# Second selective scan: the order of three instructions on TensorE and ScalarE in steps 3 and 4 of each group of eight

## The chip, the cores and the metric

One core of a Trainium2 chip. The time is the device time of one execution in microseconds (us); the kernel before was run three times.

## The reference, cut to what matters

The program is a chain of four layers on a tensor of 8 x 64 x 32 x 32: window attention with an MLP, an up- and down-sampling filter, a two-way selective scan over 8 tokens of each pixel ("scan 2"), and a selective scan over 1024 positions with an MLP ("scan 3"). The change lies in the second scan alone:

```python
def step(hst, inp):
    d_t, u_t, B_t, C_t = inp
    dA = jnp.exp(d_t[:, :, None] * A)
    hst = dA * hst + (d_t * u_t)[:, :, None] * B_t[:, None, :]
    y_t = jnp.einsum('bdn,bn->bd', hst, C_t)
    return (hst, y_t)
```

It runs over 8 tokens forward and, for the reversed sequence, backward. Here d is delta, the softplus of a projection; u is the projected input; B and C have 16 states; A is 16 x 16.

## The kernel before, in words

`scan2` (L888) works in 128 units. Eight units make a group (512 columns of pixels and tokens), and a unit covers 1024 columns of 128 (channel, state) pairs. Five engines run the same software pipeline, each in its own instruction stream: step s is written out for 16 values of u (`skewed2`, L875), the first 16 and the last 16 steps are peeled, and the rest is a loop. k = u % 8 is the place of a step in its group. The order on an engine is the order of the statements in `body`; an engine waits on semaphores and nothing behind a waiting instruction goes ahead.

What a step does:

- TensorE (L944 on). It spreads one unit's input (`ps_u`, s_pu in the trace, four matmuls: two halves of 512 columns, each the sum of a high and a low part), which needs DVE's `feed` of the unit before (semaphore `fed`); in steps k = 3 and 4 it subtracts the high part of B or of C from what stands in `ps_m` (L957, one matmul with the negated identity); it spreads the unit's delta (`ps_d`, s_pd, four matmuls, L940 as all spreads); it spreads one half of B or C into `ps_m` (`states(0)`, two matmuls; in step 3 it waits for the low part of B, in step 4 for that of C), sums products over states into `ps_y` (L1003, 16 small matmuls), spreads the other half (`states(1)`), and in k = 0 to 3 computes a projection of the next group into the same `ps_m` (L1017 to L1027: xp, delta, B, C).
- ScalarE (L1037 on). In k = 3 and 4 it copies the remainder out of `ps_m` as the low part (L1063); it takes the exponentials `fore` (L1069) and `aft` (L1074) of the spread delta, the decays of the forward and of the backward scan, with the copy of the first half of B or C (`states(0)`, L1058) between them and that of the second half (`states(1)`) behind; then come the k-dependent copies for the next group (in k = 3 the high part of C L1104, the logarithm L1106 and exp minus 1 L1108; in k = 2 the high part of B L1098 and L1100).
- DVE (L1132 on). Per unit: `feed` = spread input x B (L1140), the forward scan `ahead` (L1147, needs `fore`), the backward scan `back` (L1150, needs `aft`).
- GpSimd (L1160 on). It issues the DMA that adds `back` onto `ahead` (L1176) and multiplies the sum by C (L1173); in k = 4 to 7 it finishes delta, input and their low parts for the next group (L1179 to L1200).

PSUM holds one copy each of `ps_u`, `ps_d` and `feed` (two banks each), and of `ps_m` and `ps_y`: `ps_m` is used by every spread of B and C, by both subtractions and by every projection, one after another.

TensorE is in step s with unit s - 8 for input and delta; ScalarE takes the decays of unit s - 8 in step s; DVE works on unit s - 9. In the peeled first steps (s below 8) there is no unit yet, and from s = 128 on there is no further group. So steps 3 and 4 hold both a subtraction and a unit for units 3 and 4, 11 and 12, and so on to 115 and 116: 15 pairs, the first of them in the run-in, where the sums over states (L1003) have not begun.

Of the kernel before, what the change touches and what calls it, by code (L numbers as in the profile page):

```python
# [10 lines left out]
ACT = mybir.ActivationFunctionType  # L11
# [55 lines left out]
def live(p, n):  # L67

    return not isinstance(p, int) or 0 <= p < n
# [801 lines left out]
UNITS = 128  # L871
# [16 lines left out]
def scan2(nc, consts, x, xt, y, selr, ysel):  # L888
# [6 lines left out]
    with ExitStack() as ctx:  # L895
# [7 lines left out]
        negid = m.sb("s_negid", [P, P], F32R)  # L903
        parts_b, parts_c, parts_d, parts_u = (m.sb("s_parts" + t, [P, 2, 2, N], F32R) for t in "bcdu")
# [5 lines left out]
        ps_m, ps_y = (m.banks("s_p" + t, 1)[0] for t in "my")  # L910
# [3 lines left out]
            log_done, delta_done, du_done, b_rest, c_rest = (m.sem("s_" + t) for t in (  # L914
                "xpps", "xpd", "dtps", "bps", "cps", "awayd", "relud", "exd", "oned", "lnd", "grownd", "offd",
                "logd", "deltad", "dud", "brest", "crest"))
        hi_d, hi_u, hi_b, hi_c, lo_d, lo_u, lo_b, lo_c = (
            m.sem("s_" + t) for t in ("hid", "hiu", "hib", "hic", "lod", "lou", "lob", "loc"))
# [15 lines left out]
        @block.tensor  # L934
        def _(pe):
            pe.wait_ge(ready, 5)

            def spread(bank, sel, parts):
                for part in range(2):
                    mm = pe.matmul(bank, selr[:, sel * P:(sel + 1) * P], parts[:, part], start=(part == 0),  # L940
                                   stop=(part == 1))
                return mm

            def body(s, u):  # L944
                k, par, gi = u % 8, u // 8, s - u % 8
                p, v = s - LAG_D, u - LAG_D
                if live(p, UNITS):
                    half, j, g = place(v)
                    if v % 8 == 0:
                        pe.wait_ge(lo_u, p + 8)  # L950
                    wait(pe, fed, p)
                    for i in range(2):
                        mm = spread(ps_u[:, i * N:(i + 1) * N], 2 * (2 * j + i) + g, parts_u[:, half])
                    mm.then_inc(u_rep, 1)
                if k in (3, 4) and live(s, UNITS):
                    pe.wait_ge((hi_b, hi_c)[k - 3], gi + 8)
                    pe.matmul(ps_m[:], negid[:], (parts_b, parts_c)[k - 3][:, par, 0], start=False, stop=True,  # L957
                              skip_group_check=True).then_inc((b_rest, c_rest)[k - 3], 8)
                if live(p, UNITS):
                    if v % 8 == 0:  # L960
                        pe.wait_ge(lo_d, p + 8)
                    wait(pe, fore_done, p)
                    wait(pe, aft_done, p)
                    for i in range(2):
                        mm = spread(ps_d[:, i * N:(i + 1) * N], 2 * (2 * j + i) + g, parts_d[:, half])
                    mm.then_inc(d_ps, 1)
                q, w = s - LAG_B, u - LAG_B

                def states(i):
                    half, j, second = place(w)  # L970
                    if w % 8 == second and i == 0:
                        pe.wait_ge((lo_b, lo_c)[second], q - second + 8)
                    if i == 1:
                        pe.wait_ge((b_copied, c_copied)[second], q - second + 1)
                    else:
                        if isinstance(q, int) and q == 0:
                            pe.wait_ge(lo_c, 8)
                        if 1 <= k <= 4 and live(s, UNITS):
                            pe.wait_ge((xp_done, relu_done, lo_b, lo_c)[k - 1], gi + 8)
                        if second:  # L980
                            pe.wait_ge(b_copied, q + 1)
                        else:
                            wait(pe, c_copied, q)
                    spread(ps_m[:], 16 + 2 * j + i, (parts_b, parts_c)[second][:, half]).then_inc(
                        (b_rep, c_rep)[second], 1)

                if live(q, UNITS):
                    states(0)
                o = s - LAG_Y
                if live(o, UNITS):  # L990
                    _, j, g = place(u - LAG_Y)
                    if (u - LAG_Y) % 8 == 0:
                        wait(pe, y_done, o)
                        off = 8 * o if isinstance(o, int) else o * 8
                        for h in range(HALVES):
                            px = x[:].rearrange("p (b n) -> p b n", n=HW)[:, :, ds(off, PX)]
                            pe.matmul(ps_y[:].rearrange("p (b h n) -> p h b n", h=HALVES, n=PX)[:, h], wskip[:, h], px,
                                      start=(h == 0), stop=False, skip_group_check=True)
                    pe.wait_ge(prod_done, o + 1)
                    terms = prod[:, (u - LAG_Y) % 2].rearrange("p (n t) -> p t n", t=TOK)  # L1000
                    for odd in range(2):
                        for quad in range(4):
                            mm = pe.matmul(ps_y[quad * 32:(quad + 1) * 32, j * NPX:(j + 1) * NPX],  # L1003
                                           ysel[:, (2 * odd + g) * 32:(2 * odd + g + 1) * 32],
                                           terms[:, 2 * quad + odd], start=False, stop=(odd == 1 and g == 1),
                                           tile_position=(0, quad * 32), skip_group_check=True)
                    mm.then_inc(y_part, 1)
                if live(q, UNITS):
                    states(1)
                if k < 4 and live(s, UNITS):  # L1010
                    if live(q, UNITS):
                        if w % 2:
                            pe.wait_ge(c_copied, q + 1)
                        else:
                            pe.wait_ge(b_copied, q + 2)
                    if k == 0:
                        pe.matmul(ps_m[:], c["wxp"][:, par * P:(par + 1) * P], xt[:, ds((s - u) * 32, N)],  # L1017
                                  start=True, stop=True).then_inc(xp_ps, 8)
                    if k == 1:
                        pe.wait_ge(xp_done, gi + 8)  # L1020
                        pe.matmul(ps_m[:], wdt[:], xp[:], start=True, stop=True).then_inc(dt_ps, 8)
                    if k == 2:
                        pe.wait_ge(relu_done, gi + 8)
                        pe.matmul(ps_m[:], c["wb"], xp[:], start=True, stop=True).then_inc(b_ps, 8)
                    if k == 3:
                        pe.wait_ge(lo_b, gi + 8)
                        pe.matmul(ps_m[:], c["wc"], xp[:], start=True, stop=True).then_inc(c_ps, 8)  # L1027

            skewed2(pe, body)

        @block.scalar
        def _(act):
# [4 lines left out]
            def body(s, u):  # L1037
# [8 lines left out]
                p, v = s - LAG_D, u - LAG_D  # L1046
# [3 lines left out]
                def states(i):  # L1050
                    second, buf = w % 2, w % (4 + 4 * (w % 2)) // 2
                    if live(q, UNITS):
                        act.wait_ge((b_rep, c_rep)[second], q - second + i + 1)
                        if second:
                            wait(act, prod_done, q - 7)
                        else:
                            wait(act, fed, q - 2)
                        act.activation((bs, cs)[second][:, buf, i], ps_m[:],  # L1058
                                       ACT.Copy).then_inc((b_copied, c_copied)[second], 1)

                if k in (3, 4) and live(s, UNITS):
                    act.wait_ge((b_rest, c_rest)[k - 3], gi + 8)
                    act.activation((parts_b, parts_c)[k - 3][:, par, 1], ps_m[:],  # L1063
                                   ACT.Copy).then_inc((lo_b, lo_c)[k - 3], 8)
                if live(p, UNITS):
                    b, g = v % 2, place(v)[2]
                    act.wait_ge(d_ps, p + 1)
                    wait(act, ahead_done, p - 1)
                    act.activation(fore[:, b, :, 1:], rates[:, :, 1:], ACT.Exp,  # L1069
                                   scale=aneg[:, g:g + 1]).then_inc(fore_done, 1)  # L1070
                states(0)
                if live(p, UNITS):
                    wait(act, back_done, p - 1)
# [728 lines left out]
```

## Time and profile before

| what | value |
|---|---|
| median of 3 runs | 2016.04 us (2014.6 to 2017.21) |
| the profiled execution's own time | 2014.68 us |
| its span in the trace | 2012.7 us |
| share of the span: TensorE, DVE, ScalarE, GpSimd busy | 82%, 79%, 58%, 58% |
| first and last `feed` of the second scan | 509.0 and 1258.9 us |
| mean granted TensorE clock | 0.942 of full speed |

The span is what the trace covers; 1.98 us of the execution lie around it. The share of busy time is a mean over stages with different limits, so the scan is read by itself, between 509 and 1265 us, in order of time. A bracket behind a row gives the idle time of the engine just before the instruction and what released it.

### The profile page before, as it was taken

Reading aid. Unit: us, or ns where it says so; the run is one execution under the profiler, and the core shown is the slowest. Engines: PE = TensorE matmul, PEld = TensorE weight load, DVE = VectorE, ACT = ScalarE, POOL = GpSimd, SP = SyncE. Lnnn points to the kernel's source line nnn. Section 1 sums busy time; section 2 is a strip of 40 time slices with the busy share of each in tenths; the row PEclk is TensorE's granted clock in tenths of the full one; section 3 lists DMA queues with packets and bytes.
Section 4 is the critical chain, followed back from the end, with each engine's and each line's share of the span. In section 5 each row is a group of like instructions: output and inputs, shape, how many; then the busy total and the mean of one; then the engine's idle time right before and its main releaser. Section 6 shows DMA issues by size and latency. Waiting matters only on the chain. (4 is left out here: it accounts for less than half of the span.)

```text
span 2012.7 us, 31048 instructions
## 1 busy us (share of the span) xinstructions
PE 1651.0 (82%) x9878; PEld 979.8 (49%) x9878; DVE 1585.5 (79%) x1549; ACT 1158.2 (58%) x1889; POOL 1168.7 (58%) x881
## 2 busy tenths in 40 slices
PE   5888787996788888888888888657888888888787
PEld 2555444884444454444545544234555554554333
DVE  3788745554799999999999999441899999999854
ACT  3444484334666666666666665265666665665356
POOL 0666501001467767676776775202899999999701
PEclk8999988997899999999999999777999999999898
DMA  4000000000254444444444444200000000000001
GB/s 135 2 0 0 1 0 1 1 1 1 53 95 88 90 90 87 94 83 94 89 89 83 94 91 92 44 1 0 1 1 0 0 0 0 0 0 0 7 5 42
DMA packets 23435, 78.21 MB, mean 39 GB/s; under 512 B 3792, under 2 KB 4816, under 8 KB 23120
## 3 DMA queue, kind: packets, MB, share of 16 engines
q0 software_dynamic: 18432, 67.12, 17.6%
q1 hardware_dynamic: 4944, 10.35, 1.8%
q8 instruction: 32, 0.52, 0.1%
q14 instruction: 27, 0.22, 0.0%
HBM read 8.25 MB, written 2.10 MB: 5 GB/s over the span
## 5 line engine op out<-in xcount | busy, mean ns | idle before, releaser
L1173 POOL TENSOR_TENSOR s_prod<-s_ahead,s_cs 128x1024 f32<-128x1024 f32 x128 | 312.2, 2439 | 203.7 <-DVE s_back L1150 103.1
L1708 POOL TENSOR_TENSOR r_prod<-r_state,r_cs 128x512 f32<-128x512 f32 x256 | 322.4, 1298 | 14.8 <-DVE r_state L1649 14.2
L1147 DVE TENSOR_TENSOR_SCAN s_ahead<-s_fore,s_pfeed 128x1024 f32<-128x1024 f32 x128 | 292.7, 2287 | 11.8 <-ACT s_fore L1069 5.3
L1150 DVE TENSOR_TENSOR_SCAN s_back<-s_aft,s_pfeed 128x1024 f32<-128x1024 f32 x128 | 289.5, 2261 | 0.0
L1069 ACT ACTIVATE s_fore<-s_pd,s_aneg 128x896 f32<-128x896 f32 x128 | 129.7, 1013 | 161.0 <-PE s_pd L940 161.0
L940 PE MATMUL s_pu<-s_partsu,selr 128*128 128x512 f32 x512 | 173.4, 462 | 52.2 <-DVE s_pfeed L1140 52.0
L1636 DVE TENSOR_TENSOR r_feed<-r_pu,r_bs 128x512 f32<-128x512 f32 x256 | 164.4, 687 | 61.9 <-PE r_pu L1478 61.9
L1140 DVE TENSOR_TENSOR s_pfeed<-s_pu,s_bs 128x1024 f32<-128x1024 f32 x128 | 157.8, 1233 | 37.7 <-PE s_pu L940 25.0
L1601 ACT ACTIVATE r_decay<-r_pd,r_aneg 128x512 f32<-128x512 f32 x256 | 168.3, 686 | 23.2 <-PE r_pd L1478 23.0
L1478 PE MATMUL r_pu<-r_parts,selr 128*128 128x512 f32 x512 | 161.3, 437 | 5.7 <-DVE r_feed L1636 5.7
L1649 DVE TENSOR_TENSOR_SCAN r_state<-r_decay,r_carry,r_feed 128x512 f32<-128x512 f32 x128 | 156.3, 1263 | 0.0
L1478 PE MATMUL r_pd<-r_parts,selr 128*128 128x512 f32 x512 | 154.5, 405 | 0.0
L1003 PE MATMUL s_py<-s_prod,ysel 128*32 128x128 f32 x2048 | 142.4, 408 | 12.2 <-POOL s_prod L1173 12.2
L940 PEld LDWEIGHTS s_pu<-s_partsu,selr 128*128 128x128 f32 x512 | 95.0, 194 | 117.5 <-DVE s_pfeed L1140 73.0
L1649 DVE TENSOR_TENSOR_SCAN r_state<-r_decay,r_feed 128x512 f32<-128x512 f32 x128 | 148.6, 1202 | 0.0
L940 PE MATMUL s_pd<-s_partsd,selr 128*128 128x512 f32 x512 | 144.9, 407 | 0.0
L1478 PE MATMUL r_pm<-r_parts,selr 128*128 128x512 f32 x256 | 92.2, 443 | 57.1 <-POOL r_parts L1713 45.8
L1074 ACT ACTIVATE s_aft<-s_pd,s_aneg 128x896 f32<-128x896 f32 x128 | 129.8, 1014 | 0.0
L1478 PEld LDWEIGHTS r_pu<-r_parts,selr 128*128 128x128 f32 x512 | 93.9, 193 | 72.0 <-issue 39.2
L1176 POOL DMA_DIRECT2D s_ahead<-s_back x128 | 120.3, 940 | 14.6 <-DVE s_back L1150 14.6
L940 PEld LDWEIGHTS s_pd<-s_partsd,selr 128*128 128x128 f32 x512 | 101.0, 197 | 21.9
L1478 PEld LDWEIGHTS r_pd<-r_parts,selr 128*128 128x128 f32 x512 | 99.0, 193 | 25.1 <-issue 1.0
(255 smaller groups left out, 3338.1 us busy)
## 6 DMA issues: line engine op xcount, KB each, us to landing
s_ahead<-s_back POOLq DMA_DIRECT2D x128, 512.0 KB, 4.5
x_act<-in_x_dram SPq DMA_DIRECT2D x8, 256.0 KB, 5.4
out_dram<-x_act SPq DMA_DIRECT2D x16, 128.0 KB, 2.3
k_scan<-in_pack_scan_dram SPq DMA_DIRECT2D x1, 1600.0 KB, 10.4
k_fir<-in_pack_fir_dram SPq DMA_DIRECT2D x1, 1600.0 KB, 13.8
k_l<-in_pack_l_dram SPq DMA_DIRECT2D x1, 450.0 KB, 6.9
k_ln<-in_pack_ln_dram SPq DMA_DIRECT2D x3, 131.0 KB, 3.0
k_mlp<-in_pack_mlp_dram SPq DMA_DIRECT2D x2, 194.0 KB, 5.1
```

What stands on the lines that cost most here:

```text
L940: mm = pe.matmul(bank, selr[:, sel * P:(sel + 1) * P], parts[:, part], start=(part == 0), stop=(part == 1))
L1003: mm = pe.matmul(ps_y[quad * 32:(quad + 1) * 32, j * NPX:(j + 1) * NPX], ysel[:, (2 * odd + g) * 32:(2 * odd + g + 1) * 32], terms[:, 2 * ...
L1074: act.activation(aft[:, b, :, :TOK - 1], rates[:, :, :TOK - 1], ACT.Exp, scale=aneg[:, g:g + 1]).then_inc(aft_done, 1)
L1140: dve.tensor_tensor(feed[:], ps_u[:], bs[:, buf].rearrange("p i n -> p (i n)"), ALU.mult).then_inc(fed, 1)
L1147: dve.tensor_tensor_scan(ahead[:, v % 4], f, feed[:], 0.0, ALU.mult, ALU.add).then_inc(ahead_done, 1)
L1150: dve.tensor_tensor_scan(back[:, v % 4, ::-1], a[:, ::-1], feed[:, ::-1], 0.0, ALU.mult, ALU.add).then_inc(back_done, 1)
L1173: pool.tensor_tensor(prod[:, b], ahead[:, v % 4], cs[:, buf].rearrange("p i n -> p (i n)"), ALU.mult).then_inc(prod_done, 1)
L1478: mm = pe.matmul(bank[:], selr[:, sel * P:(sel + 1) * P], parts[:, par, which, part], start=(part == 0), stop=(part == 1))
L1601: act.activation(decay[:, v % 2, q], ps_d[q % 2][:], ACT.Exp, scale=aneg[:, v % 4:v % 4 + 1]).then_inc(decayed, 1)
L1636: dve.tensor_tensor(feed[q % 2][:], ps_u[q % 2][:], bs[:, lc, q], ALU.mult).then_inc(fed, 1)
L1649: dve.tensor_tensor_scan(state[:, b, q], decay[:, b, q], feed[q % 2][:], start, ALU.mult, ALU.add).then_inc(scanned, 1)
L1708: pool.tensor_tensor(prod[:, v % 2, q], state[:, v % 2, q], cs[:, v % UNROLL // 4, q], ALU.mult).then_inc(multiplied, 1)
```

## The change

On TensorE the spread of delta goes ahead of the subtraction of the high parts; on ScalarE the forward decays (`fore`) go ahead of the copy of the low parts. Both concern only steps k = 3 and k = 4. Nothing is added or removed, and every wait goes with its instruction.

```diff
@@ TensorE
                         mm = spread(ps_u[:, i * N:(i + 1) * N], 2 * (2 * j + i) + g, parts_u[:, half])
                     mm.then_inc(u_rep, 1)
-                if k in (3, 4) and live(s, UNITS):
-                    pe.wait_ge((hi_b, hi_c)[k - 3], gi + 8)
-                    pe.matmul(ps_m[:], negid[:], (parts_b, parts_c)[k - 3][:, par, 0], start=False, stop=True,
-                              skip_group_check=True).then_inc((b_rest, c_rest)[k - 3], 8)
-                if live(p, UNITS):
                     if v % 8 == 0:
                         pe.wait_ge(lo_d, p + 8)
                     wait(pe, fore_done, p)
...
                     mm.then_inc(d_ps, 1)
+                if k in (3, 4) and live(s, UNITS):
+                    pe.wait_ge((hi_b, hi_c)[k - 3], gi + 8)
+                    pe.matmul(ps_m[:], negid[:], (parts_b, parts_c)[k - 3][:, par, 0], start=False, stop=True,
+                              skip_group_check=True).then_inc((b_rest, c_rest)[k - 3], 8)
@@ ScalarE
-                if k in (3, 4) and live(s, UNITS):
-                    act.wait_ge((b_rest, c_rest)[k - 3], gi + 8)
-                    act.activation((parts_b, parts_c)[k - 3][:, par, 1], ps_m[:],
-                                   ACT.Copy).then_inc((lo_b, lo_c)[k - 3], 8)
                 if live(p, UNITS):
...
                     act.activation(fore[:, b, :, 1:], rates[:, :, 1:], ACT.Exp,
                                    scale=aneg[:, g:g + 1]).then_inc(fore_done, 1)
+                if k in (3, 4) and live(s, UNITS):
+                    act.wait_ge((b_rest, c_rest)[k - 3], gi + 8)
+                    act.activation((parts_b, parts_c)[k - 3][:, par, 1], ps_m[:],
+                                   ACT.Copy).then_inc((lo_b, lo_c)[k - 3], 8)
                 states(0)
```

## Rows read from the trace of the kernel before

**Rows 1.** A stretch: us, busy of PE, PEld, DVE, ACT, POOL, PEclk, DMA share, GB/s

```profile
880.00:890.00 10.00, 8.41 (x51) 5.07 (x49) 9.76 (x6) 4.36 (x7) 5.50 (x5) 0.83 0.55 105
```

**Rows 2.** The page's costliest groups: busy, mean ns, idle before and its main releaser

```profile
L1147 DVE TENSOR_TENSOR_SCAN s_ahead<-s_fore,s_pfeed 128x1024 f32<-128x1024 f32 x128 | 292.7, 2287 | 11.8 <-ACT s_fore L1069 5.3
```

**Rows 3.** Timeline (start, us, engine, line), DVE, from 901 us

```profile
901.00 1.23 DVE L1140 TENSOR_TENSOR s_pfeed<-s_pu,s_bs 128x1024 f32<-128x1024 f32 x1
...
906.84 1.23 DVE L1140 TENSOR_TENSOR s_pfeed<-s_pu,s_bs 128x1024 f32<-128x1024 f32 x1
...
908.11 2.29 DVE L1147 TENSOR_TENSOR_SCAN s_ahead<-s_fore,s_pfeed 128x1024 f32<-128x1024 f32 x1
...
910.31 2.26 DVE L1150 TENSOR_TENSOR_SCAN s_back<-s_aft,s_pfeed 128x1024 f32<-128x1024 f32 x1
...
914.48 2.29 DVE L1147 TENSOR_TENSOR_SCAN s_ahead<-s_fore,s_pfeed 128x1024 f32<-128x1024 f32 x1 [0.57 <-ACT s_fore L1069]
```

**Rows 4.** Timeline, TensorE and ScalarE in a step k = 1

```profile
892.15 1.50 PE L940 MATMUL s_pu<-s_partsu,selr 128*128 128x512 f32 x4
...
893.48 1.07 PE L940 MATMUL s_pd<-s_partsd,selr 128*128 128x512 f32 x4
...
894.60 1.01 ACT L1069 ACTIVATE s_fore<-s_pd,s_aneg 128x896 f32<-128x896 f32 x1 [1.20 <-PE s_pd L940]
```

**Rows 5.** Timeline, TensorE and ScalarE in a step k = 3

```profile
904.14 1.48 PE L940 MATMUL s_pu<-s_partsu,selr 128*128 128x512 f32 x4
...
905.53 0.48 PE L957 MATMUL s_pm<-s_partsb,s_negid 128*128 128x512 f32 x1
...
906.11 0.60 ACT L1063 ACTIVATE s_partsb<-s_pm 128x512 fp32r<-128x512 f32 x1 [0.20 <-PE s_pm L957]
...
906.77 0.72 PE L940 MATMUL s_pm<-s_partsb,selr 128*128 128x512 f32 x2
...
906.97 1.01 ACT L1069 ACTIVATE s_fore<-s_pd,s_aneg 128x896 f32<-128x896 f32 x1 [0.27 <-PE s_pd L940]
...
907.42 1.11 PE L1003 MATMUL s_py<-s_prod,ysel 128*32 128x128 f32 x16
907.88 0.59 ACT L1058 ACTIVATE s_bs<-s_pm 128x512 f32<-128x512 f32 x1
...
908.35 1.01 ACT L1074 ACTIVATE s_aft<-s_pd,s_aneg 128x896 f32<-128x896 f32 x1
...
908.52 0.73 PE L940 MATMUL s_pm<-s_partsb,selr 128*128 128x512 f32 x2
...
910.52 1.50 PE L940 MATMUL s_pu<-s_partsu,selr 128*128 128x512 f32 x4
```

**Rows 6.** Timeline, TensorE and ScalarE in the step k = 4 behind it

```profile
913.39 1.00 ACT L1069 ACTIVATE s_fore<-s_pd,s_aneg 128x896 f32<-128x896 f32 x1
...
914.22 1.11 PE L1003 MATMUL s_py<-s_prod,ysel 128*32 128x128 f32 x16
...
915.26 0.73 PE L940 MATMUL s_pm<-s_partsc,selr 128*128 128x512 f32 x2
...
915.83 0.40 PE L940 MATMUL s_pu<-s_partsu,selr 128*128 128x512 f32 x1
```

**Rows 7.** Timeline, a DVE feed and TensorE's spread of input behind it, before steps k = 3

```profile
807.38 1.23 DVE L1140 TENSOR_TENSOR s_pfeed<-s_pu,s_bs 128x1024 f32<-128x1024 f32 x1
...
808.95 1.50 PE L940 MATMUL s_pu<-s_partsu,selr 128*128 128x512 f32 x4
...
854.30 1.23 DVE L1140 TENSOR_TENSOR s_pfeed<-s_pu,s_bs 128x1024 f32<-128x1024 f32 x1
...
855.69 1.50 PE L940 MATMUL s_pu<-s_partsu,selr 128*128 128x512 f32 x4
```

**Rows 8.** Timeline, GpSimd's last piece for a group, and the spread that needs it

```profile
880.61 1.73 POOL L1200 TENSOR_TENSOR s_partsu<-s_du,s_partsu 128x512 fp32r<-128x512 f32 x1
...
884.87 1.94 PE L940 MATMUL s_pu<-s_partsu,selr 128*128 128x512 f32 x4 [1.50 <-DVE s_pfeed L1140]
```

## The prediction

> **What bounds the kernel now.** I read first how full each engine is in a stretch of the second scan. DVE is busy 9.76 of 10 us there [rows 1], so the scan goes at DVE's pace, and a change on TensorE or ScalarE counts only where DVE has to wait. The page tells how much there is to win: before all 128 forward scans DVE sat idle 11.8 us, and 5.3 us of it ended with the forward decays `fore` [rows 2]. Then I read DVE's own order of time [rows 3]: one unit takes 5.84 us (feed at 901.00, the next at 906.84); the forward scan begins 1.27 us after the feed does, the backward scan 2.20 us after that. One stall stands there: at 914.48 the forward scan had waited 0.57 us for `fore`, which had ended at 914.39 [rows 6], so 0.09 us lie between an end on ScalarE and the start on DVE that it frees. This stall costs 0.53 us against the regular pace, and I found it twice in the steady part, both in a step k = 4.
>
> Last I read how late TensorE begins a unit. Its spread of the input may start when DVE's feed of the unit before ends; call the distance the lag. In steps k = 3 it is 0.16 us (855.69 after 855.53), 0.34 us (808.95 after 808.61) [rows 7] or 1.91 us (904.14 after 902.23) [rows 3, 5]. Of the 14 groups behind the run-in six lie at 0.07 to 0.16 (0.83 together), five at 0.33 or 0.34 (1.68), one at 1.30 and two at 1.91: 7.63 us in all. TensorE and ScalarE have a cycle of their own in these steps, because `ps_m` is handed back and forth: in k = 3 spread to spread takes 6.38 us (904.14 to 910.52) [rows 5], in k = 4 5.31 us (to 915.83) [rows 6]. So k = 3 loses 0.54 us to DVE and k = 4 wins 0.53 back. That is the slack on which the change works.
>
> **Step k = 3 in the new order**, times from the start of the input spread. The delta spread no longer stands behind the subtraction. It starts as in k = 1, at 893.48 - 892.15 = 1.33, and ScalarE begins `fore` at 894.60 - 892.15 = 2.45 [rows 4]; before it was 906.97 - 904.14 = 2.83 [rows 5]. So `fore` comes 0.38 us earlier, which is the change's gain. The subtraction (0.48 us [rows 5]) follows on TensorE and is over by about 2.9, while `fore` runs: it costs nothing, and its cover is `fore`. But the low part waits on ScalarE behind `fore`. From one ScalarE instruction to the next it goes 907.88 - 906.97 = 0.91 behind a `fore`, so the low part starts at 3.36 and ends 0.60 later, at 3.96; before it ended at 2.57. Queued behind it, on both engines:
> - states(0) on TensorE, 0.06 after it (906.77 after 906.71): 4.02, over at 4.74; before 2.63.
> - The sums over states, 0.65 later: 4.67; before 3.28.
> - The copy of B's first half, 0.10 after the spread's end, as the low part stands behind the subtraction (906.11 after 906.01): 4.84; before 3.74.
> - `aft`, 0.47 behind that copy: 5.31 to 6.32; before 4.21 to 5.22.
> - states(1) stands behind the sums, which hold TensorE 1.04 us (914.22 to 915.26 [rows 6]): 5.71; before 4.38.
> - From states(1) to the next input spread 2.00 us pass (908.52 to 910.52): 7.71 instead of 6.38.
>
> So this step grows by 1.33 us. Before, the low part was copied while TensorE spread delta; now two waits in series that lay beside each other have become one chain.
>
> **Step k = 4.** The same holds up to states(1): `fore` at 2.45 (ScalarE's copies for the next group are over by 2.49, within the overlap of its instructions), `aft` from 5.31 to 6.32, states(1) at 5.71. From there the next input spread takes 0.57 us (915.26 to 915.83 [rows 6]), so the step takes 6.28 us instead of 5.31.
>
> **What DVE sees.** Let L be the lag at k = 3. At k = 4 it is L + 7.71 - 5.84 = L + 1.87. Counted from the end of the feed before, DVE wants its feed at 5.84 - 1.23 = 4.61, the forward scan at 5.88 and the backward scan at 8.08 [rows 3]. In k = 4:
> - The input spread ends at L + 1.87 + 1.50: in time for L below 1.24.
> - `fore` ends at L + 1.87 + 3.46 = L + 5.33, plus 0.09: the forward scan is met for L below 0.46.
> - `aft` ends at L + 1.87 + 6.32, plus 0.09 = L + 8.28. DVE wants it at 8.08. **The backward scan waits L + 0.20 us in every group.**
>
> The waits are one behind another, so the last one counts, not their sum. In k = 5 the lag of a group with L = 0.34 is about 2.1, no instruction is late any more, and TensorE has made the rest good by k = 7, where today it stands waiting for DVE (1.50 us at 884.87 [rows 8]). Over 14 groups: 7.63 + 14 x 0.20 = 10.4 us. The two stalls of today are in that (they are the groups with L = 1.91), so 2 x 0.53 = 1.1 us goes off: **+9.3 us**.
>
> The edits with one answer: no DMA is moved, and SP's queue is not touched. GpSimd's chain for the next group starts from ScalarE's last copy of k = 4, which comes 1.33 us later; its last piece ended at 882.34 and TensorE took it at 884.87 [rows 8], 2.5 us of cover, which remains. Were that gone, the rest (at most 1.33 us less DVE's own delay) would fall on k = 0. In the run-in the sums over states are still missing, DVE does wait for `fore` there, and `fore` comes 0.4 us earlier twice, while `aft` and the next spread come later: I take zero, with -1 and +1.5 as ends. The last steps hold no such pair.
>
> The terms that no row shows are where the handovers fall in the new order. From below: if the sums let states(1) through as soon as its copy is done, it starts at 5.5, L + 0.20 becomes about L - 0.05, and the total +5. From above: the two handovers from TensorE to ScalarE may take the 0.27 us that ScalarE waited for delta [rows 5] instead of 0.10, in two steps, some 0.4 us per group: +15. I take the middle value, since each of its pieces has a row of the same pair of instructions.
>
> The profiled execution took 2014.68 us; with +9.3 it would take 2024.0. It lies 1.36 us below the median of the three runs, 2016.04, so that I forecast 2016.04 + 9.3 = **2025.3 us**.
>
> **The clock.** In the stretch at 880 to 890 us the granted clock was 0.83, so part of it at 1.2 and part at 2.4 GHz [rows 1]; TensorE had waited 1.50 us for DVE just before its input spread, and this spread took 1.94 us instead of 1.50 [rows 4, 8]. This group is the one with L = 1.91. So one such stretch at an unlucky place costs 1.6 us of lag, of which DVE felt only 0.53; with the slack gone it would feel all.
> The Trainium skill ("TensorE: Matmul & The Clock Gate", "HAM oscillation — how this bites in real kernels") says that a TensorE that idles between bursts falls back to the slow clock again and again. The trace agrees so far as the one stretch shows. By that rule the new waits for the low parts, some 1.4 us each, would bring more slow stretches than today.
>
> **Rivals.**
> - *More slow stretches.* If each of the other 11 groups got one at the bad place: 11 x 1.6 = 18 us more, 2043 us. For it: TensorE idles longer in k = 3 and 4. Against it: it idles less in k = 5 to 7, where most of its waiting lies now, and its work is the same. Chance 0.08.
> - *The chain is hidden.* If the pieces overlap better by over half a microsecond per group, only the three groups with a long lag stall: 1.0 + 1.6 + 1.6 - 1.1 = +3.1 us, 2019.1 us, or about nothing. Against it: ScalarE keeps its order, and both `fore` and `aft` (2 x 1 us) and two copies have to pass. Chance 0.13.
> - *Faster: `fore` is what decides.* The backward scan always finds `aft` ready, as it does today, and all idle time that ended with `fore`, 5.3 us [rows 2], goes: 2010.7 us. It decides if `aft` ends before 8.08, that is if the low part, states(0) and its copy take at least 0.2 us less than I add up even in groups with the smallest lag, and over 1.9 us less in the late ones; also most of the 5.3 us lies in steps of the run-in that aren't touched. Chance 0.04.
> - *The change does not do what it says*, because in k = 4 `fore` stands behind ScalarE's copies that end at 2.49: this touches 0.04 us, and would leave the losses. It is within the forecast.
>
> **How the numbers follow.** The forecast has 0.75. A measurement of this kernel can tell about 0.2%, 4 us. The forecast's own ends, +5 to +15, give 2021 to 2031; to hold the time 8 times in 10 I reach to 2019 for the hidden chain and to 2033 for one or two more slow stretches. Slower by over 0.2%: 0.75 + 0.08 = 0.83, and with a little of the hidden chain's chance 0.84; within 0.2%: 0.12; faster by over 0.2%: 0.04.
>
> **What would show it.** In the changed profile: `fore` at 2.45 after the input spread in k = 3 and 4; the low part directly behind it; 7.7 and 6.3 us from input spread to input spread; a new line of idle time before the backward scan (today 0), ended by `aft`, some 0.3 to 0.5 us per group in k = 4, and no stall before the forward scan in the steady part. If the backward scan has no idle time the forecast is wrong, and so it is if TensorE's cycle in k = 3 stays under 7 us.

## The result, and the profile of the changed kernel

The changed kernel takes 2030.51 us (median of 6 runs, 2028.4 to 2032.29) against 2015.13 us for the kernel before in the same series: 15.4 us more, ratio 1.0075 with a 95% interval of 1.0062 to 1.0088. The forecast was 2025.3 us, 9.3 us more than before, so the measured time lies 5.2 us above it, inside the stated range of 2019 to 2033.

The page of the changed kernel has this span and these lines for the two scans (busy, mean ns, idle before and its main releaser):

```profile
span 2030.4 us, 31048 instructions
...
L1146 DVE TENSOR_TENSOR_SCAN s_ahead<-s_fore,s_pfeed 128x1024 f32<-128x1024 f32 x128 | 292.7, 2287 | 13.8 <-ACT s_fore L1064 7.4
L1149 DVE TENSOR_TENSOR_SCAN s_back<-s_aft,s_pfeed 128x1024 f32<-128x1024 f32 x128 | 289.9, 2265 | 6.9 <-ACT s_aft L1073 6.9
```

The view of who waited for whom, DVE in the second scan (us in total, times, longest):

```profile
DVE s_pfeed L1139 <- PE s_pu L940: 30.5, 7, 24.9
DVE s_ahead L1146 <- ACT s_fore L1064: 7.4, 11, 1.5
DVE s_back L1149 <- ACT s_aft L1073: 6.9, 16, 0.6
```

Before, the forward scan had waited 5.3 us for `fore` [rows 2]. The third line is the announced new one: the backward scan, which never had to wait, now waits 16 times for `aft`. 16 is 14 steady groups and the two units of the run-in (the peeled first steps). The 11 waits before the forward scan are six of the run-in and one of about 0.63 us in each of five groups that TensorE began late. In the first line the 24.9 us are the wait for the very first input (23.2 before); the other six waits, 5.6 us, are for an input spread that came late.

The steps themselves. The timeline of a regular group, k = 3 from 865.35 and k = 4 from 873.05, TensorE, ScalarE and DVE:

```profile
865.35 1.49 PE L940 MATMUL s_pu<-s_partsu,selr 128*128 128x512 f32 x4
...
866.68 1.07 PE L940 MATMUL s_pd<-s_partsd,selr 128*128 128x512 f32 x4
...
867.60 0.39 PE L964 MATMUL s_pm<-s_partsb,s_negid 128*128 128x512 f32 x1
867.79 1.01 ACT L1064 ACTIVATE s_fore<-s_pd,s_aneg 128x896 f32<-128x896 f32 x1 [0.68 <-PE s_pd L940]
868.70 0.59 ACT L1068 ACTIVATE s_partsb<-s_pm 128x512 fp32r<-128x512 f32 x1
869.34 0.73 PE L940 MATMUL s_pm<-s_partsb,selr 128*128 128x512 f32 x2 [1.36 <-ACT s_partsb L1068]
...
870.01 1.11 PE L1002 MATMUL s_py<-s_prod,ysel 128*32 128x128 f32 x16
870.11 0.60 ACT L1057 ACTIVATE s_bs<-s_pm 128x512 f32<-128x512 f32 x1 [0.82 <-PE s_pm L940]
870.61 1.01 ACT L1073 ACTIVATE s_aft<-s_pd,s_aneg 128x896 f32<-128x896 f32 x1
...
871.05 0.73 PE L940 MATMUL s_pm<-s_partsb,selr 128*128 128x512 f32 x2
...
873.05 1.49 PE L940 MATMUL s_pu<-s_partsu,selr 128*128 128x512 f32 x4
...
875.50 1.01 ACT L1064 ACTIVATE s_fore<-s_pd,s_aneg 128x896 f32<-128x896 f32 x1
...
878.38 1.01 ACT L1073 ACTIVATE s_aft<-s_pd,s_aneg 128x896 f32<-128x896 f32 x1
...
879.33 0.85 PE L940 MATMUL s_pu<-s_partsu,selr 128*128 128x512 f32 x3
879.52 2.29 DVE L1149 TENSOR_TENSOR_SCAN s_back<-s_aft,s_pfeed 128x1024 f32<-128x1024 f32 x1 [0.34 <-ACT s_aft L1073]
```

From the input spread on, `fore` comes at 2.44 (forecast 2.45, before 2.83 [rows 5]), the low part at 3.35 (3.36), states(0) (the spread of the first half) at 3.99 (4.02), its copy at 4.76 (4.84), `aft` at 5.26 (5.31), states(1) at 5.70 (5.71), and the next input spread at 7.70 (7.71, before 6.38). Step k = 4 takes 6.28 us, as forecast (873.05 to 879.33). Two brackets show the price: TensorE stands 1.36 us for the low part, and ScalarE 0.82 us for states(0), in a stretch where both had gone on before. `aft` of k = 4 ends at 879.39, and the backward scan begins at 879.52.

Where the time went, by the two profiled executions (feed times from DVE's timeline). In the 14 steady groups steps 3 and 4 cost DVE 12.9 us over the regular 5.84 per unit, against 1.0 before: +11.9. The units 0 to 5 took 42.7 us from first feed to seventh, against 40.7: +2.1. The other 3.7 us of the 17.7 us between the spans (2.2 before the first feed, 1.5 behind the last) lie in code that the change doesn't touch; this execution also lay 1.8 us above its median. 11.9 + 2.1 = 14.0 us stands against the 15.4 us of the medians.

### The profile page after: what moved, and what is told of

The parts are those of the page before. It is cut to its first block and busy times, and to the rows that moved or that the text cites. A ratio compares the mean times of both kernels' runs of the same rounds, so it can differ in the third digit from the quotient of the medians.

```text
span 2030.4 us, 31048 instructions
## 1 busy us (share of the span) xinstructions
PE 1650.8 (81%) x9878; PEld 986.8 (49%) x9878; DVE 1587.1 (78%) x1549; ACT 1161.9 (57%) x1889; POOL 1168.7 (58%) x881
## 3 DMA queue, kind: packets, MB, share of 16 engines
q0 software_dynamic: 18432, 67.12, 17.5%
## 5 line engine op out<-in xcount | busy, mean ns | idle before, releaser
L1707 POOL TENSOR_TENSOR r_prod<-r_state,r_cs 128x512 f32<-128x512 f32 x256 | 323.4, 1303 | 15.9 <-DVE r_state L1648 15.4
L940 PE MATMUL s_pm<-s_partsb,selr 128*128 128x512 f32 x256 | 89.9, 433 | 31.3 <-ACT s_partsb L1068 20.4
## 6 DMA issues: line engine op xcount, KB each, us to landing
k_fir<-in_pack_fir_dram SPq DMA_DIRECT2D x1, 1600.0 KB, 14.1
```

The costliest lines, as they stand in the source:

```text
L1707: pool.tensor_tensor(prod[:, v % 2, q], state[:, v % 2, q], cs[:, v % UNROLL // 4, q], ALU.mult).then_inc(multiplied, 1)
```

## The experiments

A group is called late when its lag L at k = 3 is 1.3 us or more, and regular otherwise; to stall is to exceed DVE's 5.84 us per unit. Theory: steps 3 and 4 are one chain of handovers of `ps_m` between TensorE and ScalarE; the low part behind `fore` lengthens it, and DVE pays L plus a constant in k = 4, L being the lag at k = 3. The constant follows from the order alone. Rivals: only the late `aft` costs something; each moved instruction has a price of its own and the prices add up; the extra time is TensorE's clock.

**Step 3 alone, step 4 alone.**

```diff
@@ TensorE, ahead of delta's spread
+                if k == 4 and live(s, UNITS):
+                    pe.wait_ge(hi_c, gi + 8)
...
@@ TensorE, behind it
-                if k in (3, 4) and live(s, UNITS):
+                if k == 3 and live(s, UNITS):
...
@@ ScalarE, the same for the low part, around fore
```

This is step 3 alone against the changed kernel; in the other kernel 3 and 4 are exchanged.

> The new order in step k = 3 alone; k = 4 as before. Theory (chain over ps_m): TensorE's cycle is 7.71 us in k = 3 and stays 5.31 in k = 4, so the unit of k = 4 begins L + 1.87 us behind its gate, and its forward decays end at 3.87 instead of 3.46 after the spread of the input: the forward scan, not the backward one, waits L - 0.05 us per group, with L the lag at k = 3 (0.15 to 0.35 in most groups, 1.3 to 1.9 where the TensorE clock fell before the group). Sum over 14 groups, with the two stalls of before taken off, +6 to +8 us, and 1 us in the run-in: about 2022 us. Rival (only the late backward decays of k = 4 cost anything, k = 3 is covered by the slack): within 2 us of before.

Measured: 2024.84 us against 2015.34, ratio 1.0043 (1.0030 to 1.0055), six runs from 2018.5 to 2028.28. The waits of DVE:

```profile
DVE s_ahead L1155 <- ACT s_fore L1073: 10.2, 14, 2.0
...
DVE s_back L1158 <- ACT s_aft L1082: 0.5, 1, 0.5
```

The wait is before the forward scan, as expected, and not before the backward one. The lags at k = 3 in the profiled execution add up to 8.45 us; L - 0.05 over 14 groups gives 7.75, and 7.75 us were found. So the rival in which only a late `aft` costs falls: step 3 alone, whose own `aft` no steady scan waits for, costs 9.5 of the 15.4 us, in the steady groups through step 4's `fore` (and, in the four late ones, its input first). The median is 2.8 us above the expected 2022. In the profiled execution the steady groups cost 7.75 less the 1.0 of before, inside the expected 6 to 8; the run-in cost 2.1 us, not 1. The rest of the 2.8 us isn't located.

> The new order in step k = 4 alone; k = 3 as before. Theory: the cycle stays 6.38 us in k = 3 and is 6.28 in k = 4; the unit of k = 4 begins only L + 0.54 behind its gate, the backward decays end 6.32 later, and DVE waits L - 1.13 us, that is nothing in the regular groups and 0.3 to 0.8 in the two to five late ones; the two stalls of 0.53 before go. Together 0 to +2 us: about 2016 us, not to be told from before. Rival (each late low part costs the same, about half of the loss per step): +7 us.

Measured: 2018.88 us against 2015.34, ratio 1.0016 (1.0007 to 1.0025), where 0 to +2 us was expected. The ten regular groups stall 0.00 us. Four late groups, with L = 1.61, 1.61, 1.72 and 1.90, stall 0.49, 0.49, 0.66 and 0.76; L - 1.13 gives 0.48, 0.48, 0.59 and 0.77. The mechanism holds, and with four late groups the scan of the profiled execution is only 1.7 us longer than before, as expected; but this execution lies 1.9 us below its median, and what makes the median 3.5 us isn't shown; more late groups in the other executions could do it. The two steps together cost 15, alone 9.5 and 3.5: with step 3 as before, step 4's new order stays within the slack of a regular group; with step 3 in the new order the slack is gone, and it turns L - 0.05 into L + 0.20.

**The run-in alone, and everything but the run-in.**

```diff
@@ TensorE and ScalarE, at the new places
-                if k in (3, 4) and live(s, UNITS):
+                if k in (3, 4) and isinstance(s, int) and s < 16 and live(s, UNITS):
...
@@ TensorE and ScalarE, at the old places
+                if k in (3, 4) and not (isinstance(s, int) and s < 16) and live(s, UNITS):
...
```

In the other kernel the two conditions are exchanged.

> The new order only in the peeled first steps (s = 11 and 12, units 3 and 4). The theory on record had zero here; the trace of the changed kernel shows units 3 to 5 taking 23.4 us instead of 20.1. Theory now: DVE waits in the run-in for TensorE, so every us of longer cycle is paid in full (1.1 in k = 3) and the late spread of unit 4 falls into a longer stretch of the slow TensorE clock: +2 to +3.5 us, about 2018 us. Rival (the clock in the run-in differs from run to run anyway, and the order costs nothing): within 1 us of before.

Measured: 2018.02 us against 2015.34 (ratio 1.0015, 1.0006 to 1.0024), +2.7 us.

> The new order everywhere but in the peeled first steps. Theory: the 14 steady groups alone cost 12 us (L + 0.20 each, with the L of the changed kernel, 1.06 taken off): about 2027 us, and with the run-in's part it adds up to the whole change, +15. Rival (the steady part costs the +9.3 on record and the run-in the rest): 2024.5 us.

Measured: 2027.83 us, ratio 1.0060 (1.0047 to 1.0073), +12.5 us, where the theory had 12 and the rival 9.3. Together 15.2 us: the two parts make up the whole change. The profile is less clear than the time: its execution has three late groups, as before has, and its steady groups stall 10.6 us (L + 0.20 gives 10.1), 9.6 us more than before. It took 12.9 us more than the profiled execution before; 2.7 us of that lie ahead of the first feed and behind the last, in code that is the same.

What happens in the run-in stands in the timeline of the changed kernel, units 3 and 4:

```profile
528.40 1.49 PE L940 MATMUL s_pu<-s_partsu,selr 128*128 128x512 f32 x4
...
534.73 2.29 DVE L1149 TENSOR_TENSOR_SCAN s_back<-s_aft,s_pfeed 128x1024 f32<-128x1024 f32 x1 [0.49 <-ACT s_aft L1073]
...
536.73 2.69 PE L940 MATMUL s_pu<-s_partsu,selr 128*128 128x512 f32 x4
...
539.47 1.23 DVE L1139 TENSOR_TENSOR s_pfeed<-s_pu,s_bs 128x1024 f32<-128x1024 f32 x1 [2.45 <-PE s_pu L940]
...
542.16 2.29 DVE L1146 TENSOR_TENSOR_SCAN s_ahead<-s_fore,s_pfeed 128x1024 f32<-128x1024 f32 x1 [1.46 <-ACT s_fore L1064]
```

and in the kernel before, TensorE's input spreads of the same two units and of unit 5:

```profile
527.39 1.50 PE L940 MATMUL s_pu<-s_partsu,selr 128*128 128x512 f32 x4
...
534.13 2.69 PE L940 MATMUL s_pu<-s_partsu,selr 128*128 128x512 f32 x4
...
540.20 1.09 PE L940 MATMUL s_pu<-s_partsu,selr 128*128 128x512 f32 x4
```

There is no slack here: DVE waits in every one of these units, so the longer step is paid at once. From the spread of unit 3 to that of unit 4 it is 8.33 us instead of 6.74, and from there to unit 5 8.22 us (to 544.95) instead of 6.07. The slow spread of unit 4, 2.69 us, is not new: it took as long before. What the run-in costs hangs on where such slow stretches fall. The kernel with the sums first, below, has the changed kernel's order in this run-in and is slow at unit 3 instead of 4 (2.63 and 1.50 us); its units 0 to 5 took 40.8 us, against 42.7 in the changed kernel, 43.3 in the one with the run-in alone, and 40.7 and 41.1 in the two with the old order there. So +2.7 us is the difference of the medians, and in a single execution it can be next to nothing. The stretch 530 to 545 us, of the changed kernel (PE, PEld, DVE, ACT, POOL, then PEclk):

```profile
530.00:545.00 15.00, 10.18 (x25) 5.78 (x24) 9.79 (x7) 8.59 (x13) 8.09 (x6) 0.75 0.19 37
```

and of the kernel before:

```profile
530.00:545.00 15.00, 12.21 (x52) 7.44 (x51) 12.15 (x7) 10.57 (x15) 10.26 (x8) 0.89 0.19 37
```

The granted clock was 0.75 instead of 0.89, that is, more of the stretch at 1.2 GHz; TensorE had waited 1.36 us for the low part in step k = 3, shortly before. That this wait brought the clock down is not shown, and two kernels speak against it: with the sums first, where TensorE waits 1.35 us at the same place, the same stretch had 0.96, and with ScalarE's half alone 0.94.

**Each engine's half alone.**

```diff
@@ TensorE's half alone, against the changed kernel
+                if k in (3, 4) and live(s, UNITS):
+                    act.wait_ge((b_rest, c_rest)[k - 3], gi + 8)
+                    act.activation((parts_b, parts_c)[k - 3][:, par, 1], ps_m[:],
+                                   ACT.Copy).then_inc((lo_b, lo_c)[k - 3], 8)
                 if live(p, UNITS):
...
-                if k in (3, 4) and live(s, UNITS):
-                    act.wait_ge((b_rest, c_rest)[k - 3], gi + 8)
...
                 states(0)
```

ScalarE's half alone has TensorE's instructions back in the old order instead, and ScalarE as in the change.

> TensorE's half alone: delta's spread ahead of the subtraction, ScalarE still copies the low part ahead of the forward decays. Theory, from the start of the input spread: subtraction at 2.25, low part 2.74 to 3.34, forward decays 3.23 to 4.24, states(0) 3.40, its copy 4.20, backward decays 4.67 to 5.68, states(1) 5.09: cycle 7.09 us in k = 3 and 5.66 in k = 4; DVE waits max(0, L - 0.30) us for the forward decays in k = 4, so 0.05 in the regular groups and 1.0 to 1.6 in two to five late ones; with the run-in +3 to +6 us, about 2020 us. Rival (the moved subtraction is what costs): the full +15 us.

Measured: 2021.64 us against 2015.60, ratio 1.0037 (1.0024 to 1.0050), +6.0. Regular groups stall 0.00 to 0.02 us, four late ones (L = 1.83, 1.73, 1.88, 1.75) 1.52, 1.42, 1.55 and 1.41, with L - 0.30 giving 1.53, 1.43, 1.58 and 1.45.

> ScalarE's half alone: the forward decays ahead of the low part, TensorE still subtracts ahead of delta's spread. Theory: forward decays at 2.83, low part 3.74 to 4.34, states(0) 4.40, backward decays 5.69 to 6.70, states(1) 6.09: cycle 8.09 us in k = 3, 6.66 in k = 4; DVE waits L + 0.96 us for the backward decays in every group: 22 us in the steady part, 3 to 5 in the run-in: about 2040 us, dearer than the whole change. Rival (the two halves add up to the whole +15): about 2025 us.

Measured: 2037.66 us against 2015.60, ratio 1.0117 (1.0102 to 1.0131), +22.1, the dearest of all. DVE's timeline in its step 4:

```profile
829.48 1.23 DVE L1140 TENSOR_TENSOR s_pfeed<-s_pu,s_bs 128x1024 f32<-128x1024 f32 x1
831.37 2.29 DVE L1147 TENSOR_TENSOR_SCAN s_ahead<-s_fore,s_pfeed 128x1024 f32<-128x1024 f32 x1 [0.65 <-ACT s_fore L1065]
834.22 2.29 DVE L1150 TENSOR_TENSOR_SCAN s_back<-s_aft,s_pfeed 128x1024 f32<-128x1024 f32 x1 [0.57 <-ACT s_aft L1074]
836.61 1.23 DVE L1140 TENSOR_TENSOR s_pfeed<-s_pu,s_bs 128x1024 f32<-128x1024 f32 x1
```

All 14 groups pay: 7.13 us instead of 5.84 here (L = 0.32; L + 0.96 = 1.28, found 1.29), 17.5 us in all, with L + 0.96 giving 16.8. The expected 2040 us took late groups as in the changed kernel; this execution had none, only one slow stretch behind a step 4 that cost 0.7 us more. 6.0 + 22.1 is far from 15.4: the halves don't add up, since TensorE's half takes the subtraction out of `fore`'s way, 0.38 us in each of the two steps, and so turns the L + 0.96 of ScalarE's half into L + 0.20. That rival falls.

**Two changes to the changed kernel.**

```diff
@@ the sums first: TensorE
-                if live(q, UNITS):
+                if live(q, UNITS) and not (k in (3, 4)):
                     states(0)
                 o = s - LAG_Y
...
                     mm.then_inc(y_part, 1)
+                if live(q, UNITS) and k in (3, 4):
+                    states(0)
                 if live(q, UNITS):
                     states(1)
@@ the decays together: ScalarE
-                states(0)
+                if not (k in (3, 4)):
+                    states(0)
                 if live(p, UNITS):
                     wait(act, back_done, p - 1)
                     act.activation(aft[:, b, :, :TOK - 1], rates[:, :, :TOK - 1], ACT.Exp,
                                    scale=aneg[:, g:g + 1]).then_inc(aft_done, 1)
+                if k in (3, 4):
+                    states(0)
                 states(1)
```

> The changed kernel, but in steps 3 and 4 TensorE does the sums over states ahead of states(0), while it waits for the low part. Theory: states(1) no longer stands behind the sums but only behind the copy of the first half, at 5.48 instead of 5.71; cycle 7.48 us in k = 3 and 6.05 in k = 4; the wait in k = 4 falls from L + 0.20 to L - 0.03, 3.2 us in 14 groups: about 2027 us. Rival (the sums aren't on the path, ScalarE's order alone decides): no difference to the changed kernel, 2030.5 us.

Measured: 2029.72 us against 2015.60, ratio 1.0073 (1.0060 to 1.0086): 14.1 us above before and not to be told from the changed kernel. The theory had 2027 and misses; by the median the rival (no difference, 2030.5) is met. The trace tells two effects apart. In the regular groups the step is shorter, and DVE waits less: a group with L = 0.34 stalls 0.24 instead of 0.54 us, one with L = 0.15 some 0.1 instead of 0.43. Its step k = 3:

```profile
815.07 1.49 PE L940 MATMUL s_pu<-s_partsu,selr 128*128 128x512 f32 x4
...
817.63 1.11 PE L1002 MATMUL s_py<-s_prod,ysel 128*32 128x128 f32 x16
...
819.06 0.73 PE L940 MATMUL s_pm<-s_partsb,selr 128*128 128x512 f32 x2 [0.32 <-ACT s_partsb L1070]
...
820.49 0.73 PE L940 MATMUL s_pm<-s_partsb,selr 128*128 128x512 f32 x2 [0.69 <-ACT s_bs L1059]
...
822.48 1.48 PE L940 MATMUL s_pu<-s_partsu,selr 128*128 128x512 f32 x4
```

7.41 us instead of 7.70, and states(1) now waits for the copy, not for the sums. But six of the 14 groups met a slow stretch of TensorE's clock in this execution, five in the changed kernel's, and each cost about 1.77 us. Four of them have L = 0.15 or less, so that L - 0.03 doesn't foretell them: in all four the input spread of step 4 itself took 2.69 us instead of 1.49, and the granted clock around it (677.5 to 684.5 us for the first) was 0.76. So in this order, in the one execution profiled, the rival of the prediction, slow stretches that fall into steps 3 and 4, takes back what the shorter step wins.

> The changed kernel, but in steps 3 and 4 ScalarE takes the backward decays ahead of the copy of the first half, into the time in which it waits for states(0). Theory: backward decays 3.86 to 4.87 instead of 5.31 to 6.32, the copy of the first half still at 4.84, cycle still 7.71 and 6.28 us. DVE no longer waits for the backward decays; it waits max(0, L - 0.46) us for the forward ones and max(0, L - 1.05) for the feed: nothing in the regular groups, 1.0 to 1.5 us in two to five late ones; run-in still +1 to +3: about 2019 us. Rival (the longer cycle costs by itself, whichever decays are late): 2028 us or more.

Measured: 2023.41 us against 2015.60, ratio 1.0039 (1.0024 to 1.0053), six runs from 2019.21 to 2029.37. A step k = 3 of it on ScalarE, and the copy that follows:

```profile
814.42 1.01 ACT L1064 ACTIVATE s_fore<-s_pd,s_aneg 128x896 f32<-128x896 f32 x1 [0.67 <-PE s_pd L940]
815.32 0.59 ACT L1068 ACTIVATE s_partsb<-s_pm 128x512 fp32r<-128x512 f32 x1
815.80 1.02 ACT L1074 ACTIVATE s_aft<-s_pd,s_aneg 128x896 f32<-128x896 f32 x1
...
816.74 0.60 ACT L1057 ACTIVATE s_bs<-s_pm 128x512 f32<-128x512 f32 x1
```

`aft` fills what had been ScalarE's wait, the copy comes no later, and the step still takes 7.69 us (811.98 to 819.67). No backward scan waits any more, the eight regular groups stall 0.00 us, and the six late ones (L from 1.48 to 1.83) stall 1.00 to 1.35, with L - 0.46 giving 1.02 to 1.37. So about half of the loss (7.8 of 15.4 us are left) was `aft`'s place behind the copy; in a regular group the longer step does not cost by itself, and the rival (2028 us or more) falls by the median, though one single run lay at 2029.37. In a late group the longer step does cost. The median is 4.4 us above the expected 2019. The profiled execution had six late groups where I had taken two to five, at about 1.2 us each; another 4.3 us of it lie behind the last feed, in code that is the same, and there its granted clock was lower (0.97 in 1600 to 1800 us, against 1.00 in the matching 200 us of before). The single runs of this kernel differ by 10 us.

**A version meant to beat both**: step 3 as before, in step 4 the new order with both decays ahead of the copy; and the same with the sums first.

```diff
@@ TensorE and ScalarE: the new order for k == 4 alone, as above, and on ScalarE
-                states(0)
+                if not (k == 4):
+                    states(0)
...
+                if k == 4:
+                    states(0)
                 states(1)
```

> Step k = 3 as before; in k = 4 the new order, with the backward decays ahead of the copy of the first half as well. A try at a version that beats both. Theory: unit 4 of a group begins L + 0.54 behind its gate, forward decays end 3.46 and backward ones 4.87 later: DVE waits max(0, L - 1.79) us, so at most 0.1 in a late group instead of the 0.53 of before, and unit 4 of the run-in gets its forward decays about 0.4 us earlier: 0.5 to 2 us faster than before, about 2014 us, less than the measurement can tell; the profile shows it as idle time before the forward scans of 4 us or less instead of 5.3, and none before the backward scans. Rival (k = 4's longer cycle of 6.28 us costs by itself): as the order in k = 4 alone, 2018.9 us.

Measured: 2014.50 us against 2015.95, ratio 1.0001 (0.9992 to 1.0010), 11 runs, ten of them from 2013.86 to 2017.46 and one at 2023.13: no difference. The DVE waits of its profiled execution:

```profile
DVE s_pfeed L1151 <- PE s_pu L940: 26.4, 3, 24.9
DVE s_ahead L1158 <- ACT s_fore L1073: 5.7, 5, 1.5
```

No stall in any of the 14 steady groups, though two had L = 1.74 and 1.56; all five waits for `fore` lie in the run-in, and they came to 5.7 us in this execution, not to the 4 or less that were expected.

> The same, and in k = 4 TensorE does the sums over states ahead of states(0). Theory: cycle 6.05 instead of 6.28 us in k = 4, which DVE never sees, so no difference to the kernel without it: about 2014 us. Rival (the sums ahead of states(0) bring more stretches of the slow TensorE clock into steps 3 and 4, as in the changed kernel with the sums first): 2 us or more above it.

Measured: 2015.08 us, ratio 0.9999 (0.9990 to 1.0008), no difference. Neither beats the kernel before by anything that can be measured. There was 1.0 us to win in the steady part, which both won in their profiled executions, and its rest is DVE's own work.

## Why the prediction was right, and where it was short

**The steps.** Every time in the working of steps 3 and 4 was met to 0.08 us, but for the subtraction, over at 2.64 instead of 2.9 and hidden as said, and the two cycles of 7.71 and 6.28 us to 0.01. The choice between 0.10 and 0.27 us for the handovers was right on the low side: from the end of states(0), 870.07, to its copy it is 0.04 us.

**The wait in every group.** L + 0.20 is confirmed in kind and nearly in size: groups with L = 0.15 stall 0.43 (0.35 by the sum), those with L = 0.34 or 0.35 stall 0.54 (0.54 by the sum). The same arithmetic with other constants gave what DVE paid in a steady group, to 0.12 us, in six other orders of the same instructions: step 3 alone, step 4 alone, each engine's half, the decays together, and step 4 with both decays ahead. With the sums first it held in the groups that no slow stretch met, and not in the four with a slow spread in step 4. The announced sign that no steady forward scan would stall holds for the regular groups alone.

**The late groups** were the first term that was too small. I took the lags of one execution before, 7.63 us with three late groups, as a property of the kernel. In the changed kernel's execution they were 9.6 us with five late groups, which by L + 0.20 is 12.4 us instead of 10.4; found were 12.9. At least part of that is chance and not the order: the kernel with everything but the run-in has the same steady part, and its profiled execution had three late groups and lags of 7.3 us. So the forecast of +9.3 fits the 9.6 us that the steady groups cost there and falls short of the 11.9 us here. That the kernel with everything but the run-in is +12.5 us by its median all the same is not explained by its profile and stays open. A late group of the changed kernel stalls three times in a row:

```profile
827.45 1.23 DVE L1139 TENSOR_TENSOR s_pfeed<-s_pu,s_bs 128x1024 f32<-128x1024 f32 x1 [0.50 <-PE s_pu L940]
829.31 2.29 DVE L1146 TENSOR_TENSOR_SCAN s_ahead<-s_fore,s_pfeed 128x1024 f32<-128x1024 f32 x1 [0.63 <-ACT s_fore L1064]
832.16 2.29 DVE L1149 TENSOR_TENSOR_SCAN s_back<-s_aft,s_pfeed 128x1024 f32<-128x1024 f32 x1 [0.56 <-ACT s_aft L1073]
```

Each wait here is counted from where the one before it had left DVE. Together they set DVE back 1.65 us at L = 1.46; L + 0.20, the lateness of the last one against the undisturbed pace, is 1.66.

**The run-in** was the second: taken at zero with +1.5 as its upper end, it costs 2.7 us by the kernel that changes it alone. Of all terms this one was wrong in kind and not only in size: a zero was put where nothing covers the longer steps. "`fore` comes 0.4 us earlier twice" was true for unit 3 only; unit 4's whole step had been pushed back by the longer step before it, and DVE there has no slack at all. The upper end counted no slow clock on top.

**Small slips in the working.** The low end was added up wrongly: states(1) at 5.5 instead of 5.71 makes L + 0.20 into about L - 0.01 and the total +6, not +5. The lag at k = 5 of a group with L = 0.34 was put at 2.1; measured, 2.6, and no instruction was late there even so. Neither moves the forecast.

**The rivals.** The hidden chain and "`fore` is what decides" fall: all 14 steady groups stall, and in each the last wait is for `aft`. More slow stretches happened a little in one execution (five late groups for three), nowhere near eleven more. The Trainium skill ("TensorE: Matmul & The Clock Gate", "HAM oscillation — how this bites in real kernels") describes a kernel whose TensorE is back at the slow clock after each of its long DMA waits. The waits added here are for ScalarE and much shorter (1.36 us), and they do not bring that: the mean granted clock was 0.939 to 0.945 in the changed kernel's six runs, against 0.940 to 0.946 in the runs of before. The GpSimd chain had the cover that it was said to have: TensorE's lag at k = 0 stayed at 0.05 to 0.15 us, and it did so in all 14 groups.

## What to carry to other kernels

When two engines hand one buffer back and forth, write down both orders instruction by instruction from the start of the step: moving the urgent consumer ahead of the handover wins once (here 0.4 us for `fore`) and delays everything behind the handover on both engines (here the next input by 1.3 us). Compare each result with the moment at which the bounding engine wants it, for every consumer and not only for the one that is seen waiting: here the one that had never waited became the bound. And a loop that lives on slack pays for irregularities of the clock as soon as the slack is gone, so count how often they come in several executions, not in one, and treat the run-in, where there was no slack here, as a term of its own.

## What was not expected

TensorE's lag at k = 3 takes few values: 0.06 to 0.2, 0.3 to 0.35, and 1.3 to 1.9 us when a stretch of the 1.2 GHz clock fell on the beginning of the group (in the kernel before, the granted clock was 0.83 in 745 to 755, 880 to 890 and 1067 to 1077 us, at the beginning of its three late groups, and 1.00 in 786 to 796 us, at that of a regular one). There are none of these in the profiled execution of ScalarE's half alone, three in that of before, six with the decays together. Their number differs between executions with the same steady order: five in the changed kernel and three in the one with everything but the run-in. Some orders with less slack also show runs 10 us apart (2018.5 to 2028.28 with step 3 alone) where the kernel before keeps within 3.3 us (2013.85 to 2017.12 in 23 runs), but the changed kernel itself keeps within 3.9. That late groups make this spread fits the granted clocks of the runs with the decays together (0.937 to 0.939 in the three above 2025 us, 0.941 to 0.945 in the three below 2022), but is not shown, with one profile for each kernel. Why the stretches fall where they fall stays open.
